# Expert masks of a macaron layer: loads in a row, a third buffer, bias rows in the first front

## The reference

```python
def ffn(x):
    scores = sigmoid(x @ gate_w.T + lb_bias)
    topw, topi = top_k(scores, 2)
    topw = topw / (topw.sum(-1) + 1e-8)
    for e in range(8):
        m = topi == e
        wmean = (topw * m).sum() / max(m.sum(), 1)
        out += where(m.any(-1), silu(x @ gw[e].T) * (x @ uw[e].T) @ dw[e].T * wmean, 0)
    return out + silu(x @ sgw.T) * (x @ suw.T) @ sdw.T
x = x + 0.5 * ffn(layernorm(x))
x = x + attention(layernorm(x))
x = x + 0.5 * ffn(layernorm(x))
```

## Time and profile before

| | |
|---|---|
| timed runs | 785.67, 785.75, 787.93 us, median 785.75 |
| profiled execution | 778.78 us |
| its span, first to last instruction | 777.0 us |
| mean granted TensorE clock | 0.949 of 2.4 GHz |
| TensorE busy | 702.9 us, 90% of the span |
| VectorE busy | 596.0 us, 77% |
| ScalarE busy | 403.5 us, 52% |
| GpSimd busy | 108.6 us, 14% |

### The profile page before, as it was taken

One profiled execution on the slowest core, in us unless ns is written; L12 is line 12 of the kernel. 1 busy time (PEld: TensorE's weight loads), 2 busy tenths in 40 slices (PEclk: granted clock), 3 DMA queues, 4 the chain that ended last, 5 costly groups with the idle time before them and its releaser, 6 DMA issues.

```text
span 777.0 us, 15840 instructions
## 1 busy us (share of the span) xinstructions
PE 702.9 (90%) x5880; PEld 369.7 (48%) x5880; DVE 596.0 (77%) x1921; ACT 403.5 (52%) x579; POOL 108.6 (14%) x90
## 2 busy tenths in 40 slices
PE   4999794849599999999999999999999886999998
PEld 3554373737234444444444444444444255554498
DVE  5667936569799999999999999999999337756411
ACT  2353231213147677777767776777677742353300
POOL 2202407051100000000000000000000002201752
PEclk9999896969579999999999999999999997999999
DMA  7002143364211010101011101100110000004463
GB/s 207 1 0 59 27 43 54 103 159 139 80 52 37 20 31 25 38 22 27 26 36 29 27 19 37 31 25 19 37 36 3 1 1 1 2 0 58 69 98 106
DMA packets 47249, 34.69 MB, mean 45 GB/s; under 512 B 13106, under 2 KB 46514, under 8 KB 47172
## 3 DMA queue, kind: packets, MB, share of 16 engines
q1 hardware_dynamic: 46596, 33.60, 18.6%
q10 hardware_dynamic: 576, 0.08, 0.1%
HBM read 23.01 MB, written 10.39 MB: 43 GB/s over the span
## 4 chain that ended last, share of the span: by engine, by line
PE 49%; DVE 13%; issue 11%; ACT 2%; DVEq 0%; ACTq 0%
PE ps L1019 46%; DVE mx L904 8%; PE ps L1024 4%; DVE mx L897 1%; ACT h_all L626 1%; DVE h_all L897 1%; DVE xn L707 1%; DVE wb L924 0%; DVE stats L695 0%; DVE mm_ L921 0%; DVE sg L839 0%; ACT osb L615 0%; DVE idle L895 0%; DVEq L132 0%; DVE mv L699 0%
## 5 line engine op out<-in xcount | busy, mean ns | idle before, releaser
L626 ACT ACTIVATE h_all<-ps 128x1024 f32<-128x1024 f32 (+3 forms) x384 | 291.2, 810 | 112.4 <-PE ps L1019 109.2
L904 DVE TENSOR_REDUCE mx<-ps 128x1 f32<-128x512 f32 (+2 forms) x352 | 223.0, 681 | 9.3 <-PE ps L1019 6.5
L1019 PE MATMUL ps<-ks,xnT_all 57*128 57x512 bf16 (+3 forms) x768 | 178.5, 336 | 14.3 <-DVE mx L897 6.4
L1019 PE MATMUL ps<-h_all,vb 128*32 128x512 f32 (+3 forms) x1536 | 163.9, 500 | 0.6 <-ACT osb L615 0.6
L1019 PE MATMUL ps<-xnT_all,ks 59*128 59x512 bf16 (+3 forms) x768 | 158.5, 331 | 3.5 <-ACT h_all L626 3.4
L897 DVE CUSTOM_DVE_ANT_0 h_all<-ps,mask_w 128x384 bf16<-128x384 f32 (+1 forms) x256 | 149.3, 618 | 2.5 <-issue 0.9
L1019 PEld LDWEIGHTS ps<-ks,xnT_all 57*128 57x128 bf16 x768 | 56.3, 94 | 142.1 <-DVE mx L897 65.1
L1019 PE MATMUL ps<-cb 64*128 64x64 bf16 (+3 forms) x1216 | 112.2, 214 | 0.0
L719 DVE TENSOR_TENSOR h_all<-ps,sg 128x512 f32<-128x512 f32 x80 | 55.1, 690 | 57.5 <-PE ps L1019 55.2
L565 ACT ACTIVATE sg<-ps 128x512 f32<-128x512 f32 x80 | 47.8, 597 | 99.0 <-PE ps L1019 91.5
L1019 PE MATMUL ps<-xnT_all,wu 128*128 128x512 f32 x160 | 86.6, 624 | 6.1 <-DVE h_all L719 6.1
(11 more groups left out here) (117 smaller groups left out, 528.3 us busy)
## 6 DMA issues: line engine op xcount, KB each, us to landing
xnT_all<-q_scr SPq DMA_DIRECT2D x64, 96.0 KB
attn<-sel_scr SPq DMA_DIRECT2D x16, 256.0 KB, 7.3
mask_odd<-sel_scr SPq DMA_DIRECT2D x16, 256.0 KB, 8.1
q_scr<-qp SPq DMA_DIRECT2D x8, 384.0 KB
ks<-k_scr SPq DMA_DIRECT2D x64, 48.0 KB
x<-in_x SPq DMA_DIRECT2D x8, 256.0 KB, 5.8
q_scr<-qp SPq DMA_DIRECT2D x8, 256.0 KB
out<-x SPq DMA_DIRECT2D x8, 256.0 KB, 4.6
```

The costliest lines, as they stand in the source:

```text
L626: act.activation(pr[:, (NSTEP * i + s) % PR_BUFS, p:HPG:SLOTS, lo:HALF], ps[:, b:b + 2, lo:HALF], ACT.Exp)\
L904: dve.tensor_reduce(m, src, AX.X, V.max).then_inc(a_out, 1)
L1019: return pe.matmul(o, l, r, start=start, stop=stop, skip_group_check=True)
```

## The change

The constants become `MASK_BUFS` = 3, `MASK_PARTS` = 4 (a tile in each step), `AHEAD` = 6, `TOPS_AT` two tiles earlier, in both FFNs, and `SLOPES_AT` = 3, which is now a group of the front and not a tile. The third mask buffer lies in `yT`, a tile of the output projection. The bias scratch moves to `yT` and `xnT`, which are free then. SyncE stores the bias rows first, then the choice, then loads the eight masks in a row, and then waits for the constants and goes on with the stores and the stacks. VectorE makes the slope parts at the end of `front(3)` of the first FFN and two bias steps in each of the four rounds behind it, each behind a hidden tile.

```diff
--- before.py
+++ after.py
@@ -86,10 +86,10 @@
 TILE_ORDER = [(c, i) for c in range(GROUPS) for i in (MT, *range(MT))]
 FRONT = (0, 1, 2, 2, 2, 2, 2, 2)
 FRONT_END = sum(FRONT)
-SEL_AT, TOPS_AT = FRONT_END + 7, FRONT_END + 12
-SLOPES_AT = FRONT_END + 14
-MASK_BUFS, MASK_PARTS = 2, 2
-AHEAD = GROUPS // 2
+SEL_AT, TOPS_AT = FRONT_END + 7, FRONT_END + 10
+SLOPES_AT = 3
+MASK_BUFS, MASK_PARTS = 3, MT
+AHEAD = 6
 
 
 def front_tiles(c):
@@ -233,7 +233,7 @@
         routed = sb("routed", [P, TILES, 2, EXPERTS])
         sel = sb("sel", [P, TILES, EXPERTS], BF16)
         selT = sb("selT", [P, 2, P], BF16)
-        mask_odd = sb("mask_odd", [P, MT, GN], BF16)
+        mask_second = sb("mask_second", [P, MT, GN], BF16)
         tot = sb("tot", [P, 2, EXPERTS])
         wmean = sb("wmean", [P, 3, EXPERTS])
         wrow = sb("wrow", [P, MT])
@@ -260,9 +260,10 @@
         rden = sb("rden", [P, QT * HPG])
         attn = sb("attn", [P, UNITS, SEQ // P, HPG * DH])
 
-        mask_even = attn[:, UNITS - MT:UNITS].rearrange("p u t e -> p (u t e)").bitcast(BF16)\
+        mask_first = attn[:, UNITS - MT:UNITS].rearrange("p u t e -> p (u t e)").bitcast(BF16)\
             .rearrange("p (m n) -> p m n", m=MT)
-        expert_mask = (mask_even, mask_odd)
+        mask_last = yT.rearrange("p a n -> p (a n)").bitcast(BF16).rearrange("p (m n) -> p m n", m=MT)
+        expert_mask = (mask_first, mask_second, mask_last)
         assert len(expert_mask) == MASK_BUFS
 
         pr = h_all[:, 0:PR_BUFS, 0:HPG, :]
@@ -277,8 +278,8 @@
         at_rows = attn[0:HEADS].rearrange("p u t e -> p (u t e)").bitcast(BF16)\
             .rearrange("p (r n) -> p r n", n=SEQ)
         bias_st = at_rows[:, 0:6, :]
-        bias_f = h_all[0:HEADS, GROUPS - 1, 0:2, :].rearrange("p a n -> p (a n)")
-        bias_r = h_all[0:HEADS, GROUPS - 1, 2:4, :].rearrange("p a n -> p (a n)")
+        bias_f = yT[0:HEADS].rearrange("p a n -> p (a n)")
+        bias_r = xnT[0:HEADS].rearrange("p a n -> p (a n)")
 
         small_loads = [(ident, "ident"), (gate_w, "gate_w"), (lb, "lb"), (rank, "rank")]
         const_loads = [(c128[:, P:8 * P], "masks"), (slope[:, 0:1], "slopes"), (qpos, "qpos")]
@@ -298,7 +299,7 @@
         s_dve = sem("s_dve")
         s_kz = sem("s_kz")
         s_ks0 = sem("s_ks0")
-        s_mask = [sem("s_mask_even"), sem("s_mask_odd")]
+        s_mask = [sem("s_mask_first"), sem("s_mask_second"), sem("s_mask_last")]
 
         def ffn_sems(n):
 
@@ -366,9 +367,6 @@
                     sp.dma_start(expert_mask[c % MASK_BUFS][k * INTER:k * INTER + INTER], src)\
                         .then_inc(s_mask[c % MASK_BUFS], 16)
 
-            store_choice(f1)
-            for c in range(AHEAD - 1):
-                load_mask(f1, c)
             sp.wait_ge(s_bst, 1)
             sp.dma_start(bias_scr[:, 0:2, :], bias_st[:, 0, None, :].broadcast_to([HEADS, 2, SEQ])).then_inc(s_bdma, 16)
             sp.dma_start(bias_scr[:, 2:5, :], bias_st[:, 1:4, :]).then_inc(s_bdma, 16)
@@ -414,15 +412,14 @@
                                  wt[w * r:w * r + w, j, :])\
                         .then_inc(a_wd[j], 16)
 
+            store_choice(f1)
+            for c in range(GROUPS):
+                load_mask(f1, c)
             sp.wait_ge(s_kz, 1)
             sp.wait_ge(s_ks0, 4)
-            for c in range(AHEAD - 1, AHEAD + 2):
-                load_mask(f1, c)
             store_parts(0, 0, 0)
             sp.wait_ge(f1.dw0, 16 * STORES)
             load_stack(0, 0, 0, 0)
-            for c in range(AHEAD + 2, GROUPS):
-                load_mask(f1, c)
             store_parts(1, 0, 1)
             sp.wait_ge(f1.dw1, 16 * STORES)
             load_stack(0, 0, 0, 1)
@@ -484,14 +481,15 @@
 
             def mask_hidden(f, n, c):
 
-                uses = (n * GROUPS + c) // MASK_BUFS + 1
+                b = c % MASK_BUFS
+                uses = n * len(range(b, GROUPS, MASK_BUFS)) + c // MASK_BUFS + 1
                 w = MT // MASK_PARTS
                 for part in range(MASK_PARTS):
                     tiles = slice(w * part, w * part + w)
                     pool.wait_ge(f.h, HT * c + 1 + w * part + w)
                     if part == 0:
-                        pool.wait_ge(s_mask[c % MASK_BUFS], 32 * uses)
-                    pool.tensor_tensor(h_all[:, c, tiles, :], h_all[:, c, tiles, :], expert_mask[c % MASK_BUFS][:, tiles, :],
+                        pool.wait_ge(s_mask[b], 32 * uses)
+                    pool.tensor_tensor(h_all[:, c, tiles, :], h_all[:, c, tiles, :], expert_mask[b][:, tiles, :],
                                        ALU.mult).then_inc(f.hm, 1)
 
             over_groups(lambda c, par, first, last: rsqrt(c, par, f1.ve, f1.xn, f1.rs))
@@ -499,11 +497,10 @@
             pool.wait_ge(f1.xn, GROUPS)
             for c in range(AHEAD):
                 mask_hidden(f1, 0, c)
-            for c in range(AHEAD):
+            for c in range(GROUPS):
                 rsqrt(c, c % 2, f1.ve2, f1.xn2, f1.rs2)
-                mask_hidden(f1, 0, AHEAD + c)
-            for c in range(AHEAD, GROUPS):
-                rsqrt(c, c % 2, f1.ve2, f1.xn2, f1.rs2)
+                if AHEAD + c < GROUPS:
+                    mask_hidden(f1, 0, AHEAD + c)
 
             pool.wait_ge(s_late, 16 * len(late_loads))
             pool.wait_ge(f1.rs2, GROUPS)
@@ -743,6 +740,10 @@
                     if not first:
                         for k in front_tiles(c - 1):
                             hidden(k)
+                            if first_ffn and c > SLOPES_AT:
+                                bias_rows(slopes[0], 2 * (c - SLOPES_AT - 1) + k - front_tiles(c - 1).start)
+                    if first_ffn and c == SLOPES_AT:
+                        slopes.append(slope_parts())
 
                 rk = rank[:, None, :].broadcast_to([P, TILES, EXPERTS])
                 pick1, pick2, s2, eq, wt = pick
@@ -810,6 +811,7 @@
                         dve.tensor_scalar(wds[:, i, :], wd[:, i, :], wrow[:, i:i + 1], None, V.mult)
                     dve.tensor_scalar(wds[:, MT, :], wd[:, MT, :], 0.5, None, V.mult).then_inc(f.wds, 1)
 
+                slopes = []
                 statistics(0, 0)
                 over_groups(front)
                 finish(GROUPS - 2, 0)
@@ -823,10 +825,6 @@
                     hidden(k)
                     if k == TOPS_AT:
                         scale_down()
-                    if first_ffn and k == SLOPES_AT:
-                        slopes = slope_parts()
-                    if first_ffn and SLOPES_AT < k <= SLOPES_AT + 8:
-                        bias_rows(slopes, k - SLOPES_AT - 1)
 
             def ffn_down(f, qkv):
                 ch = Chain(dve, f.ch_down)
```

## The result

| | before | after |
|---|---|---|
| median of the timed executions | 786.51 us (785.67 to 787.93, 4) | 748.59 us (747.74 to 750.69, 4) |
| profiled execution, its own time | 778.78 us | 747.74 us |
| span of the profile | 777.0 us | 746.0 us |
| mean granted TensorE clock | 0.949 | 0.961 |

The ratio is 0.9525 with an interval of 0.950 to 0.955: the change takes 37.9 us off the median. Between the two profiled executions it is 31.0. The difference between 37.9 and 31.0 is what has to be explained, for the profile after follows the prediction almost step by step.

What follows compares the result with a forecast made beforehand. TensorE was taken to be held up in the first FFN by late GpSimd masks and a scale-down colliding with the first. Terms carried as absolute times summed to -28.9 at T6, off the median 785.75: 756.8 us, range 750.5 to 763.

Steps and rivals of the forecast that it cites:

- Front, +1.6: First FFN's front: slope instructions and bias steps on VectorE delay xn of group 6, a loss of 1.6 us.
- Scale-down, -8.6: First FFN: scale-down two tiles earlier escapes the first GpSimd mask, gaining 6.0 us of TensorE stop and 2.6 of low clock.
- Masks and T0, T1: First FFN: six masks end at 100; T0 and T1, first two second-norm turns on TensorE, at 110.5 (-17.3) and 118.1.
- Pieces and T3: TensorE's first score pieces start at 131.4; T3, fourth turn of the second norm, comes at 134.1, -31.6 us.
- Store chain, +4.2 at T6: SyncE's chain of stores and stacks makes ScalarE's q copy of group 4 wait 4.2 us; T6, the seventh turn, at 160.4.
- Attention and the second FFN keep their time.: Behind the second norm's turns nothing changes; TensorE works 35.89 us without a gap in the second FFN's down projection.
- 7 us more in work that no profile shows: Timed median 785.75 against profiled 778.78: the extra was taken as untouched, so 28.9 came off the median whole, giving 756.8.
- the masks did not come too slowly: Rival for the mask loads: masks pace at 5.3 us rather than 4.2, T0 and T1 together 2.5 later, 759; chance 0.12.
- The chain of stores held: Against the rival that SyncE's chain of stores and stacks is 4.2 us shorter, T6 at 156.2, 752.6 us; chance 0.22.
- the first collision: Rival, first FFN: scale-down still meets the first mask, held instructions cost 7.4 instead of 2.0, clock 2.6; 764.5, chance 0.09.
- the slower case: Rival: group 0's power instruction stands behind six masks; at 11.5 us per load pair with its turn, 788; chance 0.02.
- 0.03 for a timed run that does not follow the profile: Chance 0.03 left for timed executions that behave unlike the profile; no time was given for it.

Runs made afterwards that it cites:

- repeated trace: The kernel before, unchanged, run and traced again: median 786.31 us, ratio 1.001, profiled execution 788.11.
- tops_ffn2: The kernel before with the scale-down of the second FFN alone two tiles earlier: 775.43 us against 785.7, ratio 0.9869.
- tops_late: The changed kernel with the scale-down two tiles later again, where the kernel before has it, in both FFNs: 760.82 us, ratio 0.9673.

## Why the prediction missed

Point by point, in the prediction's order. Absolute times of after are put 2.66 us later here, by how much its turn 3 came before that of the profile before (7.49 - 4.77, with 0.06 at turn 2 the other way); that is a draw, not the change (below).

- **Front, +1.6.** Right: turns 3 to 7 take 20.72 instead of 19.07, +1.65, with idle times of 0.24 and 0.70 at turns 5 and 6. The forecast's one loss of 1.8 at turn 6 came spread over several turns.
- **Scale-down, -8.6.** Right for the first FFN: -8.8 from turn 7 to down, and down starts at 94.95 + 2.66 = 97.6 (forecast 97.8). The margin was 1.6 us (70.3 to 71.88), as forecast, and held in every traced execution of the changed kernel and of its variants with the early scale-down.
- **Masks and T0, T1.** A step takes 1.11 us rather than 1.06, a mask 4.50 rather than 4.25, the sixth ends at 102.3 rather than 100, and none of it matters, for the statistics come later. T0 at 110.3 (forecast 110.5), T1 at 118.2 (118.1). The four held xn took 4.63 against 4.25 taken, so each of them waited for a step, and the 2.4 us of the bounds for an earlier end did not come.
- **Pieces and T3.** The pieces start at 131.6 (131.4). T3 comes at 136.0 instead of 134.1: behind the 1.37 us of idle time at the pieces the clock was low in this execution, which I had charged to long stops alone. The row behind the pieces and the window over it:

```profile
129.42 4.12 PE L1017 MATMUL ps<-wds,h_all 128*128 128x128 f32 x20
```

```profile
127.00:133.00 6.00, 4.63 (x35) 4.16 (x35) 4.68 (x14) 1.25 (x4) 1.01 (x1) 0.72 0.62 190
```

  Twenty matmuls take 4.12 us where they take 2.50 at the full clock, a loss of 1.6, and the window's granted clock is 0.72, so part of it is at the lower level of 1.2 GHz. Of T1 to T3 the forecast had 16.0 and the trace has 17.9.
- **Store chain, +4.2 at T6.** Right, and shown by taking it away (-3.9, -3.7). T3 to T6 takes 25.6, forecast 26.3. T6 stands at 161.7, forecast 160.4.
- **"Attention and the second FFN keep their time."** This is the step that failed. Between the two profiles it is true: T7 to the end takes 575.7 us before and 575.0 after, though as a sum of two differences that cancel (up to the first turn of the second FFN 448.9 and 450.1, its turn 2 to 3 7.5 and 5.6). But in the repeated trace, and by tops_ffn2 in most executions that were timed, the second FFN of the kernel before loses 9.1 us to the same collision of scale-down and first mask as the first, and the edit of TOPS_AT acts in both. The reason that I gave looks at the down projection alone. I priced that collision in the first FFN and did not look at the same lines in the second, where the profile shows the last scaling starting at 716.21 beside a mask that started at 716.16, an escape by a hair that called for the question what another execution does.
- **"7 us more in work that no profile shows; I take the 28.9 off it whole."** The same error in the form of a sum. The 7 us were in the path, and the change removed them. With the second collision as a term of its own, 9.1, the same working gives 785.75 - 28.9 - 9.1 = 747.8; measured were 748.6 and 747.3. (Of the 28.9 the traces have 27.6.)

The rivals: the masks did not come too slowly; the first three were loaded within 7 us (63.54 to 70.37), the others went every 4.46 us, and GpSimd had one wait of 0.91. The chain of stores held. Neither the first collision nor the slower case happened; the price of that collision adds up to 764.8 and not 764.5 (756.8 + 5.4 + 2.6), and tops_late bears it out with 7.4 us of hold and 8.0 lost in the first FFN. The case that did happen was not among them, except as the 0.03 for a timed run that does not follow the profile.

The 37.9 us, then, by what the runs isolate: the second FFN's collision 10.3 (tops_ffn2, timed). In the first FFN, from the traces, 8.8 less 1.65 up to the down projection, 11.5 from there to T1, 10.9 from T1 to T3, less 2.0 from T3 to T6: 27.6. The sum is 37.9; that it closes to the tenth is chance, since each part is known to a microsecond or so.

## What to carry to other kernels

Where the profiled execution is faster than every timed one, look in it for two engines that just miss each other before a change is priced against the median: here the difference was a part of the path which that profile didn't show. Where a constant acts in two places of a program, read the margin in both, and count a margin of under a microsecond as lost. And when a wait is taken out of a queue, price what stood in its shadow: here a chain of stores and stack loads on SyncE took some 4 us back, and moving two loads behind the stores returned 3 to 4.
